# The C row multiplied into the scanned state channel by channel, and sixteen states summed by accumulating transposes, in a two-layer Mamba and MoE kernel

## The chip, the cores and the metric

The kernel runs on one core of a Trainium2 chip. The metric is the device time of one execution in microseconds. Everything is float32.

## The reference, cut to what matters

Two layers. Layer 0 is a selective state space mixer (Mamba) beside a mixture of experts, layer 1 a bilinear attention beside another mixture of experts. The change lies in layer 0's mixer, with 4 sequences of 1024 tokens, 256 inner channels and 16 states:

```
xc = silu(causal_conv4(xs) + conv_b)              # per channel, over time
dbl = xc @ W_x                                    # 64 dt columns | 16 B columns | 16 C columns
dt = softplus(dbl[:, :64] @ W_dt + b_dt)
h_t[d, n] = exp(dt_t[d] * A[d, n]) * h_{t-1}[d, n] + dt_t[d] * xc_t[d] * B_t[n]
y_t[d]    = sum over n of h_t[d, n] * C_t[n]
out       = ((y + xc * D_param) * silu(z)) @ W_out
```

So per state n: one recurrence over time for each channel, then a multiplication by a number that depends on the token and n but not on the channel, and a sum over the 16 states.

## The kernel before, in words

One program for the five engines, each walking the same list, `plan` (made by `make_plan`), and issuing its share of each entry in that order. Nothing is reordered at run time, so an engine that waits holds up all that stands behind it in the list.

The mixer is cut into 8 chunks q (`CH`) of 512 tokens (`HALF`). A chunk has 16 steps, one per state n, so there are 128 steps N = 16 q + n (`STEPS`). Channels lie on the partitions, in two halves k of 128. Each step:

- ScalarE (`decay`, L827) writes the decays exp(dt * A) of step N + 1 into `pA` in PSUM, one 128x512 operation per half, as soon as the scan of step N has read that half (`h_ready`). After the scan of an even chunk it copies the last column of `h` into `carry` (L961).
- GpSimd (L648) multiplies `dtx` with the B row of the state into `dBx`, 128x1024, two steps deep. It waits for the scan of two steps earlier (L646). The B rows come by DMA, broadcast to all partitions, two states to a transfer (`b_group`, L837), issued by ScalarE.
- VectorE (`scan`, L1151) runs the recurrence, one `tensor_tensor_scan` of 128x512 per half, from `pA` (PSUM) and `dBx` (SBUF) to `h` (SBUF).
- TensorE (`hflip`, L734) transposes the 8 blocks of `h` into `pH` (two PSUM banks), tokens on partitions. In that layout C is a per-partition scalar, taken from `ct`.
- VectorE (`sum`, L1164) adds `pH * ct` to `acc` in SBUF: four 128x256 operations. This comes one step later: the sum of step N - 1 stands behind the scan of step N.

At a chunk boundary (step 16 q) the last sum is followed by `accT` (L748: TensorE transposes `acc` back, 8 blocks, into `pH`), and then by `y` (L1186: VectorE, two 128x512 operations that read `pH`, and one 128x1024 operation with both inputs in SBUF) and `mix_out`. The `hflip` of that step waits for `y_ready`, since `pH` is in use.

Around these, each step carries work of the mixtures of experts in two lanes, a (layer 0, later also 1) and b (layer 1, from step 55). A slot of a lane is `gate` (VectorE: two operations, L1210 and L1217), `up` (TensorE matmuls, ScalarE tanh L976 or L981) and `flip` (TensorE transposes and the down projection into `pM`; ScalarE copies `yj`, L988, and `hT`, L991). Some steps have a second slot of lane a, called c. The order within a step is written out at the top: `WITH_SECOND` and `WITH_ONE`. Behind it come the step's extras (`at(...)`): convolution, softplus, norms, routing, gathers and the combination of expert rows. `ct` is such an extra: 8 small matmuls into `pM` and a ScalarE copy. All uses of the one bank `pM` take turns (`take`, `bank_full`, `bank_read`).

Of the kernel before, what the change touches and what calls it, by code (L numbers as in the profile page):

```python
# [7 lines left out]
ALU = mybir.AluOpType  # L8
# [3 lines left out]
P = 128  # L12
NB, L = 4, 1024
CT = L // P
HALF = 512
# [13 lines left out]
GB = 2  # L29
NG = NS // GB  # L30
# [3 lines left out]
WITH_SECOND = "a scan b sum c hflip".split()  # L34
WITH_ONE = "a scan b sum hflip".split()
# [27 lines left out]
def make_plan():  # L63
# [33 lines left out]
    def mixer_front(q, s):  # L97
# [7 lines left out]
        at(s + 6, "ct", q)  # L105
# [56 lines left out]
    for b in range(NB):  # L162
# [16 lines left out]
        for piece in range(len(pieces(1, b))):  # L179
# [5 lines left out]
            ("soft", 0), ("ln", 0), ("ct", 0), ("dt", 0)]  # L185
# [28 lines left out]
    for step in range(max(end + 3, max(extras) + 1)):  # L214
# [5 lines left out]
        for what in order:  # L220
# [29 lines left out]
def program(nc, T, out):  # L250
# [10 lines left out]
    for it in plan:  # L261
        if it[0] in ("xT", "logits", "rank", "xs", "dbl", "ct", "dtr", "z", "mix_out", "gram", "pm", "wm", "attn"):
# [27 lines left out]

    carries = [sum((m // NS) % 2 == 0 for m in range(N + 1)) for N in range(STEPS)]

    with ExitStack() as ctx:
# [85 lines left out]
        dbl = sb("dbl", [R + NS, HALF])  # L379
# [4 lines left out]
        ct = sb("ct", [P, 2, HT, NS])  # L384

        bcb = sb("bcb", [P, 2, GB, HALF])
        dBx = sb("dBx", [P, 2, DK, HALF])
        h = sb("h", [P, 2, DK, HALF])
        carry = sb("carry", [P, DK, NS])
        acc = sb("acc", [P, HT, DI])  # L390
        y = sb("y", [P, DK, HALF])

# [12 lines left out]
        b_rows = [dram(f"b_rows{q}", (NS, HALF)) for q in range(CH)]  # L405
# [25 lines left out]
        def tj_of(i, k):  # L431
# [19 lines left out]
        b_loaded = [sem("b_loaded0"), sem("b_loaded1")]  # L451
        y_ready, accT_full = sem("y_ready"), sem("accT_full")
        decay_ready, dBx_ready, h_ready, hflip_full, sum_done, carried = (
            sem("decay_ready"), sem("dBx_ready"), sem("h_ready"), sem("hflip_full"), sem("sum_done"), sem("carried"))
# [47 lines left out]
        def _(sp):  # L502
            for kind, *a in plan:
# [18 lines left out]
                elif kind == "dbl":  # L522
                    q, = a
                    sp.wait_ge(bank_read, use["dbl", q])
                    sp.dma_start(b_rows[q], dbl[R:R + NS, :]).then_inc(rows_stored, 16)
# [56 lines left out]
        def _(pool):  # L582
            for kind, *a in plan:
# [50 lines left out]
                elif kind in ("decay", "scan"):  # L634
# [5 lines left out]
                    G = N // GB  # L640
                    if n == 0:
                        pool.wait_ge(dtx_ready, q + 1)
                    if N % GB == 0:
                        pool.wait_ge(b_loaded[G % 2], 16 * (G // 2 + 1))
# [7 lines left out]
        def _(pe):  # L652
# [11 lines left out]
            for kind, *a in plan:  # L664
# [48 lines left out]
                elif kind == "dbl":  # L713
# [3 lines left out]
                    for k in range(DK):  # L717
                        last = mm(pM[0:R + NS, :], w_x[:, k, 0:R + NS], xc[q % 2][:, k, :], start=(k == 0), stop=(k == DK - 1))
                    last.then_inc(bank_full, 1)
                elif kind == "ct":  # L720
                    q, = a
                    take("ct", q)
                    for c in range(HT):
                        for k in range(DK):
                            last = mm(pM[:, c * NS:(c + 1) * NS], xc[q % 2][:, k, c * P:(c + 1) * P], w_x[:, k, R + NS:],
                                      start=(k == 0), stop=(k == DK - 1))
# [559 lines left out]
```

## Time and profile before

| | |
|---|---|
| three runs | 1298.37 us median, 1295.57 to 1302.18 |
| the profiled execution | span 1307.9 us, which is all that is recorded of its time |
| VectorE busy | 1017.0 us, 78% of the span |
| TensorE busy | 929.5 us, 71%; weight loads 657.1 us, 50% |
| GpSimd and ScalarE busy | 604.3 us, 46%; 577.0 us, 44% |
| granted TensorE clock, mean | 0.840 |

The page gives the busy time of each engine and groups of instructions by line. A group's busy time counts overlapping instructions once, so it can be less than the mean of one times the count. "Idle before" is the time in which the engine stood still ahead of such an instruction, with the work that ended the wait. The 128 steps lie between 60 us and 1105 us; before them are the loads and the first chunk's front, behind them the rest of layer 1.

### The profile page before, as it was taken

What the parts mean: (1) busy time and instruction counts of PE and PEld (TensorE: products, weight loads), DVE (VectorE), ACT (ScalarE), POOL (GpSimd) and SP (SyncE); (2) the same over time, 40 slices, a digit from 0 to 9 for tenths busy, and PEclk for the clock granted to TensorE, in tenths of its full rate; (3) what the DMA queues carried; (4) which work ended last, traced back from release to release, by engine and by line L of the source; (5) the groups of instructions that cost most, each with busy time, mean ns of one, the idle gap of its engine ahead of it and who ended that gap; (6) DMA issues with size and microseconds to landing.
All of it is one profiled execution on the core that took longest, in us unless ns stands there. A gap on an engine that the chain in (4) does not pass through costs nothing. (4 is left out here: it accounts for less than half of the span.)

```text
span 1307.9 us, 16996 instructions
## 1 busy us (share of the span) xinstructions
PE 929.5 (71%) x4484; PEld 657.1 (50%) x4484; DVE 1017.0 (78%) x2059; ACT 577.0 (44%) x1499; POOL 604.3 (46%) x416
## 2 busy tenths in 40 slices
PE   1467788776677869777887788776877887563680
PEld 0244465554455646554664565564645665432350
DVE  4398889899988998888979987889788998341333
ACT  1333545453446544644555554544464464221320
POOL 0238225675335434673255324864656363423405
PEclk9996789978888978988989998887987899675755
DMA  8812112133112212333222222343422332411404
GB/s 266 231 41 89 44 54 87 62 107 110 56 54 77 79 48 74 92 113 105 64 71 84 73 68 67 97 115 87 117 86 71 110 115 73 121 44 61 135 24 113
DMA packets 149770, 117.19 MB, mean 90 GB/s; under 512 B 15104, under 2 KB 137008, under 8 KB 149680
## 3 DMA queue, kind: packets, MB, share of 16 engines
q1 hardware_dynamic: 132272, 65.76, 17.8%
q10 hardware_dynamic: 9216, 33.56, 7.8%
q0 software_dynamic: 8192, 16.79, 4.0%
q8 instruction: 41, 0.67, 0.2%
q14 instruction: 49, 0.40, 0.1%
HBM read 76.74 MB, written 39.32 MB: 89 GB/s over the span
## 5 line engine op out<-in xcount | busy, mean ns | idle before, releaser
L648 POOL TENSOR_TENSOR dBx<-dtx,bcb 128x1024 f32<-128x1024 f32 x128 | 303.4, 2373 | 398.1 <-DVE h L1162 333.6
L1183 DVE SCALAR_TENSOR_TENSOR acc<-pH,ct,acc 128x256 f32<-128x256 f32 x480 | 197.3, 472 | 4.7 <-remote 3.3
L746 PE MATMUL pH<-const,h 128*128 128x128 f32 x1024 | 160.2, 303 | 43.9 <-DVE h L1162 15.1
L808 PE MATMUL pM<-const,hj 128*128 128x128 f32 (+3 forms) x588 | 125.3, 314 | 75.2 <-ACT hT L991 30.8
L620 POOL DMA_INDIRECT gy<-rows_out,slots x128 | 128.3, 1003 | 99.9 <-DMA rows_out<-yj 63.4
L607 POOL DMA_INDIRECT rows_in<-xn,slots x128 | 132.8, 1038 | 90.2 <-DVE expert L1108 58.3
L1162 DVE TENSOR_TENSOR_SCAN h<-pA,carry,dBx 128x512 f32<-128x512 f32 x128 | 157.0, 1268 | 19.9 <-ACT pA L835 13.6
L835 ACT ACTIVATE pA<-dt,am 128x512 f32<-128x512 f32 x256 | 167.3, 695 | 5.2 <-DVE h L1162 5.1
L1162 DVE TENSOR_TENSOR_SCAN h<-pA,dBx 128x512 f32<-128x512 f32 x128 | 149.2, 1207 | 20.9 <-ACT pA L835 12.0
L746 PEld LDWEIGHTS pH<-const,h 128*128 128x128 f32 x1024 | 126.8, 155 | 65.0 <-issue 27.8
L988 ACT ACTIVATE yj<-pM 128x128 f32<-128x128 f32 x248 | 69.3, 279 | 193.7 <-PE pM L818 170.7
L808 PEld LDWEIGHTS pM<-const,hj 128*128 128x128 f32 (+3 forms) x588 | 73.0, 148 | 152.1 <-issue 121.6
L794 PE MATMUL pG<-w13a,xgT 128*128 x184 | 88.1, 565 | 69.6 <-DVE hj L1217 65.9
L818 PE MATMUL pM<-w2b,hT 128*128 (+1 forms) x496 | 117.9, 341 | 7.1 <-ACT hT L991 4.9
L1210 DVE SCALAR_TENSOR_TENSOR hj<-tj,pG 128x352 f32<-128x352 f32 (+2 forms) x147 | 65.8, 448 | 68.0 <-ACT tj L981 41.4
L991 ACT ACTIVATE hT<-pM 128x256 f32<-128x256 f32 (+1 forms) x248 | 104.6, 422 | 0.5 <-PE pM L808 0.2
L818 PEld LDWEIGHTS pM<-w2b,hT 128*128 128x128 f32 x496 | 86.8, 218 | 33.8 <-issue 18.0
L818 PE MATMUL pM<-w2a,hT 128*128 x552 | 85.1, 295 | 0.0
L795 PE MATMUL pU<-w13a,xgT 128*128 x184 | 82.6, 535 | 0.0
L818 PEld LDWEIGHTS pM<-w2a,hT 128*128 128x128 f32 x552 | 78.5, 214 | 0.3
L794 PEld LDWEIGHTS pG<-w13a,xgT 128*128 128x128 f32 x184 | 32.4, 217 | 91.5 <-issue 91.1
L976 ACT ACTIVATE tj<-pG 128x352 f32<-128x352 f32 x92 | 42.8, 465 | 80.8 <-PE pG L794 68.1
(172 smaller groups left out, 1510.3 us busy)
## 6 DMA issues: line engine op xcount, KB each, us to landing
bcb<-b_rows ACTq DMA_DIRECT2D x64, 512.0 KB
rows_out<-yj SPq DMA_DIRECT2D x248, 64.0 KB
xg<-rows_in SPq DMA_DIRECT2D x184, 64.0 KB
rows_in<-gy SPq DMA_DIRECT2D x8, 512.0 KB, 5.6
mixed<-s_st SPq DMA_DIRECT2D x16, 256.0 KB
so<-rows_out SPq DMA_DIRECT2D x8, 512.0 KB
sr<-mixed SPq DMA_DIRECT2D x8, 512.0 KB
w13a<-in_L_ffn_w SPq DMA_DIRECT2D x2, 1408.0 KB, 8.1
```

The costliest lines, as they stand in the source:

```text
L607: pool.indirect_dma_start(rows_in[l][b % 2], bass.IndirectOffsetOnAxis(ap=slots[l][b][:, c, k:k + 1], axis=0), xn[:, c, :], None).then_inc ...
L620: pool.indirect_dma_start(gy[:, k, c, :], None, rows_out[l][b], bass.IndirectOffsetOnAxis(ap=slots[l][b][:, c, k:k + 1], axis=0)).then_inc ...
L648: pool.tensor_tensor(dBx[:, N % 2], dtx[q % 2][:], row, ALU.mult).then_inc(dBx_ready, 1)
L746: last = pe.transpose(pH[:, half, c * DI + k * P:c * DI + (k + 1) * P], h[:, N % 2, k, t * P:(t + 1) * P], ident)
L794: mm(pG[:, 0:hid], tok, w[:, 0:hid], start=True, stop=True).then_inc(gate_full, 1)
L795: mm(pU[:, 0:hid], tok, w[:, hid:2 * hid], start=True, stop=True).then_inc(gu_full[i], 1)
L808: last = pe.transpose(pM[0:w, m * P:(m + 1) * P], hj[i][:, k % 2, m * P:m * P + w], ident)
L818: last = mm(pM[:, YA:YA + P], hT[i][0:wd, m * P:(m + 1) * P], w[0:wd, m, :], start=(m == 0), stop=(m == len(ks) - 1))
L835: A(pA[:, k, :], dt[q % 2][:, k, :], ACT.Exp, scale=am[:, k, n:n + 1]).then_inc(decay_ready, 1)
L991: last = A(hT[i][:, 0:w], pM[:, 0:w], ACT.Copy)
L1162: dve.tensor_tensor_scan(h[:, N % 2, k, :], pA[:, k, :], dBx[:, N % 2, k, :], carry[:, k, n:n + 1] if q % 2 else 0.0, ALU.mult, ALU.add).t ...
L1183: last = dve.scalar_tensor_tensor(out=acc[:, t, :], in0=src, scalar=cn, in1=acc[:, t, :], op0=ALU.mult, op1=ALU.add)
```

## The change

- The C rows are stored to DRAM beside the B rows, and a transfer per step brings both rows of one state, broadcast to all partitions, into a ring of three (`BCR`). Before, one transfer brought the B rows of two states. A step now moves 512 KB instead of 256 KB, in 128 instead of 64 issues from ScalarE's queue. `ct` with its matmuls and copy goes.
- The scan writes in place, over `pA`. Behind each half's scan VectorE waits for it and multiplies the half by the C row into `hc`, one 128x512 operation. The `sum` entry goes.
- `hflip` transposes `hc` with accumulation: the 16 states of a chunk add up in `pH`. TensorE no longer waits for sums, and VectorE no longer reads `pH` in each step.
- ScalarE's decay of step N + 1 waits for the multiplication (`hc_ready`) instead of the scan, and in even chunks it first copies the last column of each half out of `pA`, with a wait for that copy.
- At the boundary, `accT` moves from the place of the sum to the place ahead of `y`, behind slot c. ScalarE copies the 128x1024 sums from `pH` to SBUF (over `y`, once `zsilu` has read it), TensorE transposes them back, and `y` follows as before.

```diff
-WITH_SECOND = "a scan b sum c hflip".split()
-WITH_ONE = "a scan b sum hflip".split()
+WITH_SECOND = "a scan b c hflip".split()
+WITH_ONE = "a scan b hflip".split()
...
-        at(s + 6, "ct", q)
...
-            elif what == "sum" and 0 < step <= STEPS:
-                plan.append(("sum", step - 1))
-                if n == 0:
-                    plan.append(("accT", q - 1))
             elif what == "hflip":
                 if step and n == 0 and step <= STEPS:
+                    plan.append(("accT", q - 1))
                     plan.append(("y", q - 1))
...
-                    row = bcb[:, G % 2, N % GB:N % GB + 1, :].broadcast_to([P, DK, HALF])
+                    row = bcb[:, N % BCR, 0:1, :].broadcast_to([P, DK, HALF])
...
-                    pe.wait_ge(h_ready, 2 * (N + 1))
+                    pe.wait_ge(hc_ready, 2 * (N + 1))
                     if n == 0 and q:
                         pe.wait_ge(y_ready, q)
                     for half in range(2):
-                        if N:
-                            pe.wait_ge(sum_done, 2 * (N - 1) + half + 1)
                         for c in range(2):
                             for k in range(DK):
                                 t = 2 * half + c
-                                last = pe.transpose(pH[:, half, c * DI + k * P:c * DI + (k + 1) * P], h[:, N % 2, k, t * P:(t + 1) * P], ident)
-                        last.then_inc(hflip_full, 1)
+                                last = mm(pH[:, half, c * DI + k * P:c * DI + (k + 1) * P], hc[:, N % 2, k, t * P:(t + 1) * P], ident,
+                                          is_transpose=True, start=(n == 0 and c == k == 0), stop=(n == NS - 1), skip_group_check=True)
+                    last.then_inc(hflip_full, 1)
                 elif kind == "accT":
                     q, = a
-                    pe.wait_ge(sum_done, 2 * NS * (q + 1))
+                    pe.wait_ge(acc_copied, q + 1)
...
+                keeps = N and (N - 1) // NS % 2 == 0
                 for k in range(DK):
                     if N:
-                        act.wait_ge(h_ready, 2 * (N - 1) + k + 1)
+                        act.wait_ge(hc_ready, 2 * (N - 1) + k + 1)
+                    if keeps:
+                        A(carry[:, k, (N - 1) % NS:(N - 1) % NS + 1], pA[:, k, HALF - 1:HALF], ACT.Copy).then_inc(carried, 1)
+                        act.wait_ge(carried, 2 * ((N - 1) // (2 * NS) * NS + (N - 1) % NS) + k + 1)
                     A(pA[:, k, :], dt[q % 2][:, k, :], ACT.Exp, scale=am[:, k, n:n + 1]).then_inc(decay_ready, 1)
...
+            def bc_load(N):
+
+                q, n = divmod(N, NS)
+                if n == 0:
+                    act.wait_ge(rows_stored, 16 * (q + 1))
+                if N >= BCR:
+                    act.wait_ge(dBx_ready, N - BCR + 1)
+                    act.wait_ge(hc_ready, 2 * (N - BCR + 1))
+                src = bc_rows[q].rearrange("(w n) t -> n w t", w=2)[n:n + 1]
+                act.dma_start(bcb[:, N % BCR], src.broadcast_to([P, 2, HALF])).then_inc(bc_loaded[N % BCR], 16)
...
+                elif kind == "accT":
                     q, = a
+                    act.wait_ge(hflip_full, NS * (q + 1))
+                    act.wait_ge(zs_ready, q + 1)
+                    A(yT.rearrange("p c d -> p (c d)"), pH[:].rearrange("p h t -> p (h t)"), ACT.Copy).then_inc(acc_copied, 1)
...
                     if N >= 2:
-                        dve.wait_ge(hflip_full, 2 * (N - 1))
-                        dve.wait_ge(carried, carries[N - 2])
...
+                        dve.wait_ge(hflip_full, N - 1)
                     for k in range(DK):
                         dve.wait_ge(decay_ready, 2 * N + k + 1)
-                        dve.tensor_tensor_scan(h[:, N % 2, k, :], pA[:, k, :], dBx[:, N % 2, k, :],
+                        dve.tensor_tensor_scan(pA[:, k, :], pA[:, k, :], dBx[:, N % 2, k, :],
                                                carry[:, k, n:n + 1] if q % 2 else 0.0, ALU.mult, ALU.add).then_inc(h_ready, 1)
-                elif kind == "sum":
...
+                        dve.wait_ge(h_ready, 2 * N + k + 1)
+                        dve.tensor_tensor(hc[:, N % 2, k, :], pA[:, k, :], bcb[:, N % BCR, 1, :], ALU.mult).then_inc(hc_ready, 1)
```

## Rows read from the trace of the kernel before

**Rows 1.** Windows, the steps: length, PE, PEld, DVE, ACT, POOL busy, clock, DMA, GB/s.

```profile
60.00:1105.00 1045.00, 807.53 (x4055) 578.96 (x4056) 922.15 (x1827) 517.88 (x1329) 534.46 (x344) 0.87 0.26 81
```

**Rows 2.** Waits of VectorE from 60 to 1105 us: total, times, longest us.

```profile
DVE h L1162 <- ACT pA L835: 25.6, 26, 2.1
...
DVE h L1162 <- PE pH L746: 3.4, 1, 3.4
```

**Rows 3.** Groups by line and shape, VectorE: busy us, mean ns, idle before.

```profile
L1183 DVE SCALAR_TENSOR_TENSOR acc<-pH,ct,acc 128x256 f32<-128x256 f32 x480 | 197.3, 472 | 4.7 <-remote 3.3 <-PE pH L746 1.3
L1162 DVE TENSOR_TENSOR_SCAN h<-pA,carry,dBx 128x512 f32<-128x512 f32 x128 | 157.0, 1268 | 19.9 <-ACT pA L835 13.6 <-issue 3.2 <-POOL dBx L648 3.0
L1162 DVE TENSOR_TENSOR_SCAN h<-pA,dBx 128x512 f32<-128x512 f32 x128 | 149.2, 1207 | 20.9 <-ACT pA L835 12.0 <-POOL dBx L648 4.8 <-PE pH L746 3.4
L1217 DVE TENSOR_TENSOR hj<-hj,pU 128x352 f32<-128x352 f32 x92 | 47.9, 521 | 10.3 <-ACT xgT L969 5.4 <-remote 1.4 <-PE pU L795 0.8
...
L1217 DVE TENSOR_TENSOR hj<-hj,p 128x176 f32<-128x176 f32 x78 | 26.3, 337 | 2.7
...
L1191 DVE SCALAR_TENSOR_TENSOR y<-xc,dpar,pH 128x512 f32<-128x512 f32 x16 | 11.2, 744 | 8.6 <-PE pH L753 8.2 <-issue 0.3
```

**Rows 4.** Timeline of VectorE, one step: start us, length us, instructions.

```profile
607.73 2.33 DVE L1162 TENSOR_TENSOR_SCAN h<-pA,dBx 128x512 f32<-128x512 f32 x2
609.98 1.63 DVE L1183 SCALAR_TENSOR_TENSOR acc<-pH,ct,acc 128x256 f32<-128x256 f32 x4
```

**Rows 5.** Line L725, the matmuls of `ct`, in the groups of TensorE.

```profile
L725 PE MATMUL pM<-w_x,xc 128*128 128x16 f32 x128 | 16.9, 275 | 0.8 <-ACT v L928 0.8
```

**Rows 6.** Timelines of ScalarE behind slot c and of VectorE at `y`, step 16.

```profile
195.07 0.48 ACT L991 ACTIVATE hT<-pM 128x384 f32<-128x384 f32 x1
...
190.70 1.41 DVE L1191 SCALAR_TENSOR_TENSOR y<-xc,dpar,pH 128x512 f32<-128x512 f32 x2 [0.21 <-PE pH L753]
192.14 1.22 DVE L1194 SCALAR_TENSOR_TENSOR y<-y,zs 128x1024 f32<-128x1024 f32 x1
```

**Rows 7.** Timeline of TensorE at step 16: `accT`, `hflip`, `mix_out`.

```profile
189.56 1.09 PE L753 MATMUL pH<-const,acc 128*128 128x128 f32 x8 [2.31 <-DVE acc L1183]
...
194.70 1.04 PE L746 MATMUL pH<-const,h 128*128 128x128 f32 x8
195.70 2.02 PE L761 MATMUL pM<-w_out,y 128*128 128x128 f32 x16
```

**Rows 8.** Timelines at step 96: ScalarE behind slot c, VectorE, GpSimd.

```profile
862.15 0.48 ACT L991 ACTIVATE hT<-pM 128x384 f32<-128x384 f32 x1
...
859.55 1.41 DVE L1191 SCALAR_TENSOR_TENSOR y<-xc,dpar,pH 128x512 f32<-128x512 f32 x2 [0.31 <-issue]
860.99 6.67 DVE L1194 SCALAR_TENSOR_TENSOR y<-y,zs 128x1024 f32<-128x1024 f32 x1
...
860.07 1.92 POOL L629 TENSOR_TENSOR gy<-gy,wts 128x1024 f32<-128x1024 f32 x1
861.93 2.35 POOL L648 TENSOR_TENSOR dBx<-dtx,bcb 128x1024 f32<-128x1024 f32 x1
864.23 2.35 POOL L633 TENSOR_TENSOR gy<-gy 128x1024 f32<-128x1024 f32 x1
```

**Rows 9.** Groups of ScalarE: the decays, and an operation of 128x1024.

```profile
L835 ACT ACTIVATE pA<-dt,am 128x512 f32<-128x512 f32 x256 | 167.3, 695 | 5.2 <-DVE h L1162 5.1
...
L933 ACT ACTIVATE ca<-v 128x1024 f32<-128x1024 f32 x8 | 8.5, 1060 | 0.3
```

**Rows 10.** Timelines at step 112, which has no slot c: ScalarE, VectorE.

```profile
1010.82 0.38 ACT L991 ACTIVATE hT<-pM 128x256 f32<-128x256 f32 x1
...
1012.55 0.75 DVE L1191 SCALAR_TENSOR_TENSOR y<-xc,dpar,pH 128x512 f32<-128x512 f32 x1 [3.84 <-PE pH L753]
```

**Rows 11.** Timeline of VectorE at step 64: the last operation of `y`.

```profile
580.56 4.20 DVE L1194 SCALAR_TENSOR_TENSOR y<-y,zs 128x1024 f32<-128x1024 f32 x1
```

**Rows 12.** Waits of GpSimd from 60 to 1105 us.

```profile
POOL dBx L648 <- DVE h L1162: 333.6, 70, 10.6
```

More of the change, by code:

```diff
@@ L261, in program @@
     for it in plan:
-        if it[0] in ("xT", "logits", "rank", "xs", "dbl", "ct", "dtr", "z", "mix_out", "gram", "pm", "wm", "attn"):
+        if it[0] in ("xT", "logits", "rank", "xs", "dbl", "dtr", "z", "mix_out", "gram", "pm", "wm", "attn"):
             takes(*it)
@@ L289, in program @@
     wide_before = [sum(2 * HID[j[0], j[2]] > 512 for j in lanes[0][:k]) for k in range(len(lanes[0]) + 1)]
-    carries = [sum((m // NS) % 2 == 0 for m in range(N + 1)) for N in range(STEPS)]
     with ExitStack() as ctx:
@@ L378, in program @@
         v = sb("v", [P, DK, HALF])
-        dbl = sb("dbl", [R + NS, HALF])
+        dbl = sb("dbl", [R + 2 * NS, HALF])
         zs = sb("zs", [P, DK, HALF])
@@ L403, in dram @@
             return nc.dram_tensor(name, shape, F32, kind="Internal").ap()
-        b_rows = [dram(f"b_rows{q}", (NS, HALF)) for q in range(CH)]
+        bc_rows = [dram(f"bc_rows{q}", (2 * NS, HALF)) for q in range(CH)]
         rows_in = [[dram(f"rows_in{l}{i}", (TILES * P, P)) for i in range(2)] for l in range(2)]
@@ L450, in program @@
             sem("rows_stored"), sem("act_chain"), sem("ln_ready"), sem("dt_ready"), sem("dtx_ready"))
-        b_loaded = [sem("b_loaded0"), sem("b_loaded1")]
+        bc_loaded = [sem(f"bc_loaded{i}") for i in range(BCR)]
         y_ready, accT_full = sem("y_ready"), sem("accT_full")
-        decay_ready, dBx_ready, h_ready, hflip_full, sum_done, carried = (
-            sem("decay_ready"), sem("dBx_ready"), sem("h_ready"), sem("hflip_full"), sem("sum_done"), sem("carried"))
+        decay_ready, dBx_ready, h_ready, hc_ready, hflip_full, carried = (
+            sem("decay_ready"), sem("dBx_ready"), sem("h_ready"), sem("hc_ready"), sem("hflip_full"), sem("carried"))
+        zs_ready, acc_copied = sem("zs_ready"), sem("acc_copied")
         mixed_stored, gathered, fetched, combined, mid_stored, out_stored = (
@@ L717, in _ @@
                     for k in range(DK):
[L718 to L726, printed above, removed]
+                        last = mm(pM[0:R + 2 * NS, :], w_x[:, k, :], xc[q % 2][:, k, :], start=(k == 0), stop=(k == DK - 1))
                     last.then_inc(bank_full, 1)
@@ L745, in _ @@
                                 t = 2 * half + c
[L746 to L747 removed]
+                                last = mm(pH[:, half, c * DI + k * P:c * DI + (k + 1) * P], hc[:, N % 2, k, t * P:(t + 1) * P], ident,
+                                          is_transpose=True, start=(n == 0 and c == k == 0), stop=(n == NS - 1), skip_group_check=True)
+                    last.then_inc(hflip_full, 1)
                 elif kind == "accT":
                     q, = a
[L750 removed]
+                    pe.wait_ge(acc_copied, q + 1)
                     for k in range(DK):
                         for c in range(HT):
[L753 removed]
+                            last = pe.transpose(pH[:, k, c * P:(c + 1) * P], yT[:, c, k * P:(k + 1) * P], ident)
                     last.then_inc(accT_full, 1)
@@ L947, in _ @@
                 elif kind == "decay":
-                    b_group(0)
-                    b_group(1)
+                    for N in range(BCR):
+                        bc_load(N)
                     act.wait_ge(prepared, 2)
@@ L956, in _ @@
                         decay(N + 1)
-                    if N % GB == GB - 1 and N // GB + 2 < CH * NG:
-                        b_group(N // GB + 2)
-                    if q % 2 == 0:
-                        act.wait_ge(h_ready, 2 * N + 2)
-                        A(carry[:, :, n], h[:, N % 2, :, HALF - 1], ACT.Copy).then_inc(carried, 1)
+                    if N + BCR < STEPS:
+                        bc_load(N + BCR)
                 elif kind == "up":
@@ L1149, in _ @@
                     dve.wait_ge(bank_read, use["z", q, 1])
-                    link(dve.scalar_tensor_tensor(out=zs[:], in0=zs[:], scalar=1.0, in1=y[:], op0=ALU.add, op1=ALU.mult))
+                    dve.scalar_tensor_tensor(out=zs[:], in0=zs[:], scalar=1.0, in1=y[:], op0=ALU.add, op1=ALU.mult).then_inc(zs_ready, 1)
+                    dve.wait_ge(zs_ready, q + 1)
                 elif kind == "scan":
@@ L1154, in _ @@
                     dve.wait_ge(dBx_ready, N + 1)
+                    if q % 2:
+                        dve.wait_ge(carried, 2 * (q // 2 * NS + n + 1))
                     if N >= 2:
[L1156 to L1159 removed]
+                        dve.wait_ge(hflip_full, N - 1)
                     for k in range(DK):
                         dve.wait_ge(decay_ready, 2 * N + k + 1)
[L1162 removed]
+                        dve.tensor_tensor_scan(pA[:, k, :], pA[:, k, :], dBx[:, N % 2, k, :],
                                                carry[:, k, n:n + 1] if q % 2 else 0.0, ALU.mult, ALU.add).then_inc(h_ready, 1)
[L1164 to L1185 removed]
+                        dve.wait_ge(h_ready, 2 * N + k + 1)
+                        dve.tensor_tensor(hc[:, N % 2, k, :], pA[:, k, :], bcb[:, N % BCR, 1, :], ALU.mult).then_inc(hc_ready, 1)
                 elif kind == "y":
```

53 lines of the change are left out of this document (8 added, 45 removed).

## The prediction, made before the changed kernel was built or run

> **What bounds the kernel now.** I read the windows first. In the stretch of the 128 steps, 1045 us of the 1307.9, VectorE is busy for 922.2 us, 88%, and TensorE for 807.5 us, 77%, at a mean granted clock of 0.87 [rows 1]. So VectorE sets the pace, with 122.8 us of idle time, about 1 us per step, and TensorE is not far behind. Its granted clock moves between the two levels of 1.2 and 2.4 GHz. Next come VectorE's waits. The largest is for the decays (25.6 us), and the wait that the round trip through TensorE causes is small, 3.4 us [rows 2]. The four sum operations cost VectorE their own time, not a wait. The groups give that time [rows 3], and the timeline of a step shows the order in which it is spent [rows 4].
>
> **VectorE's own work.** The sums are 512 operations: 197.3 us for 480 of them, 0.411 us each with their overlap [rows 3]. In a step they take 1.63 us [rows 4], of which 0.08 us overlaps with a neighbour, since the sum starts at 609.98 and the scans end at 610.06. That is 1.55 us per step, 198 us in all.
>
> Two multiplications per step come in, 128x512, one input in PSUM, one in SBUF. None of this shape is in the trace. The nearest rows are `tensor_tensor` at L1217, also one input in each: 521 ns for 352 elements and 337 ns for 176, so 1.045 ns per element and 153 ns fixed, 688 ns for 512. From above it is bounded by L1191, 512 elements with a per-partition scalar besides, 744 ns, and from below by the busy time per element alone, 535 ns [rows 3]. I take 688 ns, as its rows have the same operation. The two scans of a step overlap by 0.07 us (2.33 us for two of 1.20) [rows 3, 4]. Each multiplication must wait for its own scan, so that overlap goes. I allow 0.05 us per step for it and the waits together. Added: 2 x 0.688 + 0.05 = 1.43 us per step, 183 us. Net: **-15 us**. With 535 ns it would be -54, with 744 ns 0.
>
> The Trainium skill (VectorE: DVE Perf Modes, section on the TRN2 errata) has a table by which an operation out of PSUM takes 120 cycles plus its elements at 0.96 GHz, 658 ns here, and beside it a measured (N + 151)/0.96 for fp32 `tensor_tensor`, 691 ns. The trace's slope and constant agree with the second. By the table alone this term would be 8 us lower.
>
> The scan now writes to PSUM instead of SBUF. The trace has no scan that does. Nearest is what an extra operand costs a scan, 1268 against 1207 ns with `carry` [rows 3]. So I bound it by -0.06 and +0.06 us for each of 256 scans, 16 us either way, and take 0.
>
> **Round trips.** VectorE no longer waits for `hflip` before a sum nor TensorE for the sum: 3.4 us of VectorE's idle time [rows 2], and TensorE gets ahead by a little. I take **-5 us** (bounds 0 and -10). The `ct` matmuls take 16.9 us of TensorE [rows 5] with a turn of `pM`. TensorE is not what ends most waits, so **-3 us** (bounds 0 and -17).
>
> ScalarE is 50% busy [rows 1]. Its decay now waits for the multiplication. That is covered: the first half's decay runs while VectorE does the second half's scan and multiplication (1.9 us), against a decay of 0.7 us [rows 9] and a copy of one column. If the cover fails, the price is the 25.6 us row growing. The added issues for B and C rows (64 more) are also on its queue, behind the decay. The transfers double by 33.5 MB in a DMA system that is 26% busy [rows 1]. They are wanted two steps later. I take 0 for both, and +10 us as the upper bound.
>
> **The boundary.** Before, `accT` stood ahead of slot c, and `y` could run as soon as gate c was done: at step 16 it waited 0.21 us and started at 190.70 [rows 6]. Now TensorE's `accT` waits for a ScalarE copy that stands behind all of slot c in ScalarE's queue. That slot can only run after gate c. ScalarE's last copy for it ended at 195.55 at step 16 [rows 6], 4.85 us behind `y`'s old start, and at step 96 at 862.63, 3.08 us behind 859.55 [rows 8]. Six boundaries have a slot c (16, 32, ... 96), and over the six this mean is 3.2 us. To it come the copy, 1.06 us as another 128x1024 operation [rows 9], the 8 transposes, 1.09 us [rows 7], and 0.15 us of handing over. 0.3 us comes off, since `accT` no longer stands ahead of slot c in TensorE. So VectorE waits 5.2 us at each of six boundaries, **31 us**, with nothing to do, because the extras and the next gate stand behind `y` in its queue. TensorE waits too: `hflip`, which ran at 194.70 without a wait [rows 7], has to wait for `y`.
>
> Steps 112 and 128 have no slot c. At 112, ScalarE's copies end at 1011.20, and `y` started at 1012.55 after a wait of 3.84 us [rows 10]. Copy, transposes (up to twice 1.09 us, at the lower of the two clock levels) and the handing over put it at about 1014.5, 1.9 us later. The sum's 1.6 us that I have counted as gained were hidden there, so 3.5 us each, **7 us**.
>
> Against it: at steps 64 and 96 the last operation of `y` took 4.20 and 6.67 us [rows 8, 11], where it takes 1.22 at step 16 [rows 6]. It ended 1.08 us after the third of GpSimd's operations did [rows 8]. Started 5 us later it would not meet them: **-8 us**. And after a long wait of VectorE the other engines are ahead, so the next waits shrink: **-4 us**. Boundary in all: **+26 us**, bounds +10 and +41.
>
> **Contention with GpSimd.** The same row shows the rule: a VectorE operation with both inputs in SBUF stands still while GpSimd multiplies. The sums, with one input in PSUM, kept their 472 ns. GpSimd's `dBx` takes 2.35 us [rows 8] and starts at the end of a scan in 70 of 128 steps [rows 12]. The sums covered 1.63 us of it with work that does not mind. The multiplications cover 0.69, the second half's, so 0.94 us more of it falls on what comes next. About 50 steps have an extra with both inputs in SBUF there (convolution two steps per chunk, `xc`, `dt`, `zsilu`, the norms, the combinations): 50 x 70/128 x 0.94 = 26 us, of which I take three quarters, **+20 us**, for the waits that it shortens in turn. Bounds 0 and 47 (all 50 steps).
> The Trainium skill (SBUF — State Buffer, "Who interferes with whom") calls this an exclusive lock that the first comer holds for its whole instruction. By that the multiplication itself, with one input in SBUF, is free of it, and all 26 us would be paid, 6 more than I take.
>
> **Lane b.** Gate b stands behind the scans, so it comes 1.43 us later, and TensorE's work for b then runs into slot c. Eleven steps have both (56, 60, ... 96). At most 1.43 us each, 16 us. I take **+5 us**.
>
> Sum: -15 - 5 - 3 + 26 + 20 + 5 = +28 us on the profiled 1307.9 us. Its span is 9.5 us (0.7%) above the median of the runs, 1298.37. I carry the difference over to the median: **1326 us**.
>
> **Rivals.**
> *A, the waits are refunded (faster).* VectorE has 123 us of idle time in the steps [rows 1]. If what the boundary, lane b and GpSimd cost comes back as shorter waits for decays and tanh within the next steps, only -15 - 5 - 3 = -23 us are left: 1275 us. It decides once 5 us of boundary wait are made good within five steps of 1 us idle each. For it: after a boundary wait TensorE and ScalarE are ahead. Against it: TensorE stands still for `y` as well. Chance 0.20.
> *D, half refunded.* Half of the 51 us comes back: 1300 us, no change. Chance 0.14.
> *B, the scan in PSUM costs.* +16 us for the scans, and the whole 26 us of contention, +6, and half of the bound for DMA and ScalarE, +5: 1353 us. For it: three accesses in PSUM and SBUF per element. Against: reading from PSUM showed no extra in rows 3. Chance 0.12.
> *C, the accumulating transposes run as full matmuls.* The change would then not do what it says, a transpose. 8 transposes take 1.04 us, while the 8 matmuls of `mix_out`, of the same size, are 16 records in 2.02 us [rows 7]: +0.98 us per step on TensorE, 125 us, of which its idle time hides about half. 1326 + 62 = 1388 us. The Trainium skill (Perfetto Trace Analysis, "Transposes") says that transposes have logic that skips arithmetic. The operands here are the same as before, only the accumulation differs. Chance 0.04.
> *Forecast.* 1326 us, own range 1308 to 1345. Chance 0.50.
>
> No change means within 0.5% of 1298.37, 1292 to 1305, about what runs can tell. Faster is A, 0.20. Same is D, 0.14. Slower is the rest, 0.66. The range takes in half of A and all but C and the upper part of B: 1284 to 1354 us.
>
> **What the changed profile would show.** The multiplication at 0.69 us, 256 times. Scans at 1.20 and 1.27 us. `y` preceded by 4 to 6 us of idle time on VectorE at six boundaries, released by `accT`. `hflip` with 8 records of a transpose's length. VectorE's busy time about equal to 1017 us, its idle time in the steps up by some 25 us. Convolution, `xc` and norm operations longer than before by what falls into `dBx`. The prediction is wrong if the boundaries show less than 2 us of wait, if the two-input operations are no longer than before, or if scan and multiplication together take clearly less than 3.7 us a step.

## The result, and the profile after

The changed kernel takes 1344.71 us (median of 4 runs, 1340.59 to 1351.45), the kernel before on the same chip 1296.97 us: a ratio of **1.037 [1.0328, 1.0412]**, slower, 48 us. I had forecast 1326 us, slower, with 1308 to 1345 as my own range, so the time stands at its very edge. Chips differ by over 1% (the kernel before took 1315 us on another), so every experiment below is a ratio to the kernel before on its own chip: runs 1 to 4 shared one chip, 5 to 8 a second, 9 to 12 a third. The ratios leave out one execution of run 1 (1397.69 us) and one of run 8 (1303.07 us) that fell in a slower state.

The page of the kernel after, its span and busy times:

```profile
span 1345.6 us, 16371 instructions
## 1 busy us (share of the span) xinstructions
PE 913.9 (68%) x4356; PEld 648.3 (48%) x4356; DVE 1032.6 (77%) x1803; ACT 598.9 (45%) x1563; POOL 606.8 (45%) x416
```

Its stretch of the 128 steps, columns as in rows 1:

```profile
60.00:1145.00 1085.00, 790.23 (x3901) 569.64 (x3902) 929.66 (x1559) 534.69 (x1378) 538.70 (x344) 0.86 0.43 108
```

The steps take 1085 us where they took 1045 [rows 1]. VectorE is busy for 7.5 us more in them (929.7 against 922.2) and idle for 32.5 us more (155.3 against 122.8). Over the whole span VectorE's busy time is 1032.6 us against 1017.0. The groups of VectorE (busy us, mean ns, idle before, and what ended it) say what of it is new:

```profile
L1150 DVE TENSOR_TENSOR hc<-pA,bcb 128x512 f32<-128x512 f32 x256 | 177.0, 692 | 8.8
L1147 DVE TENSOR_TENSOR_SCAN pA<-pA,carry,dBx 128x512 f32<-128x512 f32 x128 | 164.4, 1285 | 22.2 <-POOL dBx L639 14.3 <-ACT pA L821 5.9 <-ACT carry L819 1.9
L1147 DVE TENSOR_TENSOR_SCAN pA<-pA,dBx 128x512 f32<-128x512 f32 x128 | 156.6, 1223 | 27.0 <-ACT pA L821 19.5 <-POOL dBx L639 7.3
L1107 DVE SCALAR_TENSOR_TENSOR ca<-xs,cw,ca 128x512 f32<-128x512 f32 x48 | 53.3, 1112 | 11.9 <-ACT ca L893 10.8
...
L1135 DVE SCALAR_TENSOR_TENSOR zs<-zs,y 128x1024 f32<-128x1024 f32 x8 | 23.7, 2967 | 0.0
L1117 DVE SCALAR_TENSOR_TENSOR xc<-v,ca 128x1024 f32<-128x1024 f32 x8 | 20.2, 2521 | 1.1 <-ACT v L899 1.1
...
L1156 DVE SCALAR_TENSOR_TENSOR y<-xc,dpar,pH 128x512 f32<-128x512 f32 x16 | 11.2, 744 | 52.2 <-PE pH L735 52.2
...
L1159 DVE SCALAR_TENSOR_TENSOR y<-y,zs 128x1024 f32<-128x1024 f32 x8 | 10.6, 1320 | 0.3
```

The same groups of the kernel before, where they are not among its rows above:

```profile
L1122 DVE SCALAR_TENSOR_TENSOR ca<-xs,cw,ca 128x512 f32<-128x512 f32 x48 | 43.0, 897 | 11.9 <-ACT ca L906 10.8
...
L1150 DVE SCALAR_TENSOR_TENSOR zs<-zs,y 128x1024 f32<-128x1024 f32 x8 | 19.0, 2369 | 3.0 <-ACT y L946 3.0
L1194 DVE SCALAR_TENSOR_TENSOR y<-y,zs 128x1024 f32<-128x1024 f32 x8 | 18.2, 2278 | 0.3
L1132 DVE SCALAR_TENSOR_TENSOR xc<-v,ca 128x1024 f32<-128x1024 f32 x8 | 14.2, 1774 | 1.1 <-ACT v L912 1.1
```

The multiplication takes 692 ns, 256 times, 177.0 us. The scans are 16 ns longer each than in rows 3, and have 321.0 us of busy time against 306.2. Convolution (L1107), `zsilu` (L1135) and `xc` (L1117) read both inputs from SBUF and grew by 10.3, 4.7 and 6.0 us, with unchanged counts. `y*zs` (L1159), which reads both from SBUF too, fell by 7.6 us. Ahead of `y` (L1156) there are now 52.2 us of idle time, where rows 3 have 8.6.

The timeline of VectorE at step 16 (start us, length us, idle time before in brackets) shows one of the eight waits that make these 52.2 us, and ScalarE and TensorE at the same place show what it waits for:

```profile
196.23 1.29 DVE L1147 TENSOR_TENSOR_SCAN pA<-pA,carry,dBx 128x512 f32<-128x512 f32 x1 [1.43 <-ACT carry L819]
197.56 0.69 DVE L1150 TENSOR_TENSOR hc<-pA,bcb 128x512 f32<-128x512 f32 x1
198.17 1.28 DVE L1147 TENSOR_TENSOR_SCAN pA<-pA,carry,dBx 128x512 f32<-128x512 f32 x1
...
200.63 0.52 DVE L1182 TENSOR_TENSOR hj<-hj,pU 128x352 f32<-128x352 f32 x1
209.81 1.41 DVE L1156 SCALAR_TENSOR_TENSOR y<-xc,dpar,pH 128x512 f32<-128x512 f32 x2 [8.65 <-PE pH L735]
211.25 1.23 DVE L1159 SCALAR_TENSOR_TENSOR y<-y,zs 128x1024 f32<-128x1024 f32 x1
```

```profile
206.35 0.48 ACT L976 ACTIVATE hT<-pM 128x384 f32<-128x384 f32 x1
206.72 1.03 ACT L910 ACTIVATE y<-pH 128x1024 f32<-128x1024 f32 x1
...
207.80 1.97 PE L735 MATMUL pH<-const,y 128*128 128x128 f32 x8 [1.67 <-ACT y L910]
212.62 0.66 PE L727 MATMUL pH<-const,hc 128*128 128x128 f32 x2 [2.85 <-DVE y L1159]
```

Gate c is VectorE's last work before the wait (200.63 plus 0.52). ScalarE's `hT` of slot c ends at 206.83, the copy at L910 runs until 207.75, then the transposes at L735, and `y` starts at 209.81. The eight idle times are 8.65, 5.55, 7.16, 5.58, 6.65, 6.58, 7.04 and 4.98 us. They were 0.21, 1.45, 0.20, 0.23, 0.54, 0.31, 3.84 and 1.78.

The waits of VectorE, then those of GpSimd, from 60 to 1145 us (total, times, longest), and the queue and the issue that load the B and C rows (packets, MB, share; KB, us to landing):

```profile
DVE y L1156 <- PE pH L735: 47.2, 7, 8.7
DVE pA L1147 <- ACT pA L821: 25.4, 21, 3.5
DVE pA L1147 <- POOL dBx L639: 21.6, 7, 6.5
```

```profile
POOL dBx L639 <- DVE pA L1147: 272.2, 49, 16.5
POOL dBx L639 <- DMA bcb<-bc_rows: 180.7, 37, 44.6
```

```profile
q10 hardware_dynamic: 34816, 67.12, 22.1%
...
bcb<-bc_rows ACTq DMA_DIRECT2D x128, 512.0 KB, 5.1
```

The same wait and the same queue in the kernel before:

```profile
POOL dBx L648 <- DMA bcb<-b_rows: 62.5, 7, 42.9
...
q10 hardware_dynamic: 9216, 33.56, 7.8%
```

The wait for decays has not moved (25.6 us in rows 2). The rows were the last thing that GpSimd's product waited for 7 times, and are now 37 times, 180.7 us in all. The queue has 22.1% where it had 7.8%. The bytes doubled, but the packets went from 9216 to 34816: two neighbouring B rows lay in one run of 4 KB, and a state's B row and C row lie apart, in runs of 2 KB. So the change also halved the length of the runs.

### The profile page after: what moved, and what is told of

Same layout as the page of the kernel before. It is cut to its first block and busy times, and to the rows that moved or that the text cites. A ratio compares the mean times of both kernels' runs of the same rounds, so it can differ in the third digit from the quotient of the medians.

```text
span 1345.6 us, 16371 instructions
## 1 busy us (share of the span) xinstructions
PE 913.9 (68%) x4356; PEld 648.3 (48%) x4356; DVE 1032.6 (77%) x1803; ACT 598.9 (45%) x1563; POOL 606.8 (45%) x416
## 3 DMA queue, kind: packets, MB, share of 16 engines
q10 hardware_dynamic: 34816, 67.12, 22.1%
q1 hardware_dynamic: 132400, 66.02, 17.3%
## 5 line engine op out<-in xcount | busy, mean ns | idle before, releaser
L727 PE MATMUL pH<-const,hc 128*128 128x128 f32 x1024 | 162.3, 310 | 74.9 <-DVE hc L1150 53.9
L1150 DVE TENSOR_TENSOR hc<-pA,bcb 128x512 f32<-128x512 f32 x256 | 177.0, 692 | 8.8
L1147 DVE TENSOR_TENSOR_SCAN pA<-pA,carry,dBx 128x512 f32<-128x512 f32 x128 | 164.4, 1285 | 22.2 <-POOL dBx L639 14.3
L821 ACT ACTIVATE pA<-dt,am 128x512 f32<-128x512 f32 x256 | 172.9, 693 | 15.4 <-DVE hc L1150 11.1
L1147 DVE TENSOR_TENSOR_SCAN pA<-pA,dBx 128x512 f32<-128x512 f32 x128 | 156.6, 1223 | 27.0 <-ACT pA L821 19.5
L727 PEld LDWEIGHTS pH<-const,hc 128*128 128x128 f32 x1024 | 131.5, 159 | 94.7 <-DVE hc L1150 63.2
L600 POOL DMA_INDIRECT rows_in<-xn,slots x128 | 135.7, 1060 | 73.6 <-DVE expert L1093 41.7
L790 PE MATMUL pM<-const,hj 128*128 128x128 f32 (+3 forms) x588 | 123.8, 311 | 52.2 <-DVE hj L1182 32.8
L776 PEld LDWEIGHTS pG<-w13a,xgT 128*128 128x128 f32 x184 | 32.1, 215 | 102.4 <-issue 101.9
```

Source lines behind the costliest of these rows:

```text
L600: pool.indirect_dma_start(rows_in[l][b % 2], bass.IndirectOffsetOnAxis(ap=slots[l][b][:, c, k:k + 1], axis=0), xn[:, c, :], None).then_inc ...
L727: last = mm(pH[:, half, c * DI + k * P:c * DI + (k + 1) * P], hc[:, N % 2, k, t * P:(t + 1) * P], ident, is_transpose=True, start=(n == 0 ...
L776: mm(pG[:, 0:hid], tok, w[:, 0:hid], start=True, stop=True).then_inc(gate_full, 1)
L790: last = pe.transpose(pM[0:w, m * P:(m + 1) * P], hj[i][:, k % 2, m * P:m * P + w], ident)
L821: A(pA[:, k, :], dt[q % 2][:, k, :], ACT.Exp, scale=am[:, k, n:n + 1]).then_inc(decay_ready, 1)
L1147: dve.tensor_tensor_scan(pA[:, k, :], pA[:, k, :], dBx[:, N % 2, k, :], carry[:, k, n:n + 1] if q % 2 else 0.0, ALU.mult, ALU.add).then_in ...
```

## The experiments

**1. `accT` early.** The copy and `accT` are planned ahead of slot c, as `accT` was before.

```diff
-WITH_SECOND = "a scan b c hflip".split()
+WITH_SECOND = "a acc scan b c hflip".split()
...
+            elif what == "acc":
+                if step and n == 0 and step <= STEPS:
+                    plan.append(("accT", q - 1))
```

> The changed kernel with one edit: accT (ScalarE's copy of the sums and TensorE's transposes back) stands ahead of the scan in the boundary step instead of behind slot c. Theory (the boundary wait is the largest part of the loss): the idle time ahead of y, 52.2 us in the changed kernel and 8.6 before, falls to under 12 us, and most of it, 25 to 40 us, comes off the total: 1305 to 1320 us. Rival A (boundary waits are made good within some steps): the idle time goes and the total stays within 8 us of 1345.

Measured: 1306.16 us, 1.0073 [1.0042, 1.0103]. Its groups of VectorE:

```profile
L1161 DVE SCALAR_TENSOR_TENSOR y<-y,zs 128x1024 f32<-128x1024 f32 x8 | 21.6, 2702 | 0.3
...
L1158 DVE SCALAR_TENSOR_TENSOR y<-xc,dpar,pH 128x512 f32<-128x512 f32 x16 | 11.2, 744 | 8.7 <-PE pH L737 8.6
```

`y` waits 8.7 us, as before the change, and `y*zs` is back in GpSimd's way, 21.6 us. The net is 1.037 less 1.0073, 3.0%: **38 us of the 48 are the boundary**, as my theory for the run had it (25 to 40 us).

**2. GpSimd's product in halves.** Each half waits for its own half of the scan, so it starts one scan earlier and holds SBUF in shorter pieces.

```diff
-                    if N >= 2:
-                        pool.wait_ge(h_ready, 2 * (N - 1))
-                    row = bcb[:, N % BCR, 0:1, :].broadcast_to([P, DK, HALF])
-                    pool.tensor_tensor(dBx[:, N % 2], dtx[q % 2][:], row, ALU.mult).then_inc(dBx_ready, 1)
+                    for k in range(DK):
+                        if N >= 2:
+                            pool.wait_ge(h_ready, 2 * (N - 2) + k + 1)
+                        pool.tensor_tensor(dBx[:, N % 2, k, :], dtx[q % 2][:, k, :], bcb[:, N % BCR, 0, :], ALU.mult).then_inc(dBx_ready, 1)
```

> The changed kernel with one edit: GpSimd's dBx product is made in two halves of 512, each half once the scan of two steps earlier has read that half. Half of it then runs beside the multiplication and the second scan, which have at most one input in SBUF, and only some 0.5 us instead of 1.7 us runs beside what follows. Theory (contention with GpSimd's product costs about 34 us of VectorE's busy time): convolution (53.3 us), xc (20.2) and zs (23.7) get shorter, in all 15 to 25 us off the total, 1320 to 1330. Rival: those operations are long because of GpSimd's other work, or stalls there are slack: within 5 us of 1345.

Measured: 1322.61 us, 1.0203 [1.0165, 1.024]. The page and two groups:

```profile
PE 901.5 (68%) x4356; PEld 641.5 (49%) x4356; DVE 1000.5 (76%) x1803; ACT 599.5 (45%) x1563; POOL 635.1 (48%) x544
...
L1107 DVE SCALAR_TENSOR_TENSOR ca<-xs,cw,ca 128x512 f32<-128x512 f32 x48 | 44.6, 931 | 11.9 <-ACT ca L893 10.8
...
L1117 DVE SCALAR_TENSOR_TENSOR xc<-v,ca 128x1024 f32<-128x1024 f32 x8 | 15.3, 1909 | 1.1 <-ACT v L899 1.1
```

VectorE's busy time falls by 32.1 us, and convolution and `xc` go back nearly to what they were before the change (43.0 and 14.2 us). That looked like a measure of the contention that the change exposed, until run 6.

**3. Rows side by side.** A state's B row and C row lie next to each other in DRAM, so the same bytes go in runs of 4 KB instead of 2, as they did before the change.

```diff
-        bc_rows = [dram(f"bc_rows{q}", (2 * NS, HALF)) for q in range(CH)]
+        bc_rows = [dram(f"bc_rows{q}", (NS, 2, HALF)) for q in range(CH)]
```

> The changed kernel with one edit: B row and C row of a state lie side by side in DRAM (stored by two DMAs per chunk), so a broadcast moves 4 KB runs instead of 2 KB runs, same bytes. Theory (the DMA term, taken as nothing in the prediction, is real: GpSimd waits 181 us for the rows, and VectorE 21.6 us for dBx against 7.8): the queue's share falls from 22% to about 15%, the transfers land sooner than 5.1 us, the wait of VectorE for dBx falls under 14 us, total 5 to 12 us lower, 1333 to 1340. Rival (DMA is hidden by the two steps of lead): same time within 4 us.

Measured: 1343.56 us, 1.0348 [1.0297, 1.0398], no difference from the kernel after. GpSimd's wait for rows fell to 102.1 us, 19 times, and VectorE's for `dBx` only to 17.9, where my theory had under 14. The page's queue and issue:

```profile
q10 hardware_dynamic: 18432, 67.12, 15.2%
...
bcb<-bc_rows ACTq DMA_DIRECT2D x128, 512.0 KB, 3.8
```

**4. Thin rows.** From the fourth step on only 16 of 128 partitions are loaded with B and C.

```diff
-                act.dma_start(bcb[:, N % BCR], src.broadcast_to([P, 2, HALF])).then_inc(bc_loaded[N % BCR], 16)
+                p = P if N < BCR else 16
+                act.dma_start(bcb[0:p, N % BCR], src.broadcast_to([p, 2, HALF])).then_inc(bc_loaded[N % BCR], 16)
```

> The changed kernel with one edit: from the fourth step on, only 16 of the 128 partitions of the B and C rows are loaded (the others keep what the first three loads brought, so the sums are not the reference's). It leaves out seven eighths of the added and the old row traffic. If waiting for rows and DMA load cost something, this is its upper bound: GpSimd's waits for the rows go from 181 us to about the 43 us of the start, VectorE's wait for dBx to under 9 us, total 10 to 20 us lower (1325 to 1335). Rival (hidden): within 4 us of 1345.

Measured: 1331.91 us, 1.0257 [1.0222, 1.0291]. This kernel's output is not the reference's. All but an eighth of the row traffic, the old B rows' share included, is worth 1.1%, 12 us below run 3 and 15 by the two ratios (their intervals leave 8 to 22). VectorE's wait for `dBx` stays at 20.5 us, so rows that come late are not its cause. VectorE's busy time is 10 us lower, 1022.5, and GpSimd hardly ever finds the rows late:

```profile
POOL dBx L639 <- DVE pA L1148: 386.5, 76, 17.3
POOL dBx L639 <- DMA bcb<-bc_rows: 51.6, 4, 44.3
```

**5 and 6. Both edits together, and the split in the kernel before.** Run 5 is 1 and 2 in one kernel. Run 6 has edit 2 alone in the kernel before the change.

> The changed kernel with both edits of the first runs: accT ahead of the scan, and GpSimd's product in halves. Theory (boundary wait and contention are separate losses and add): 1345 - 38 - 22 = 1285 us, 0.6 to 1.3% faster than the kernel before. Rival (they share idle time, so that the second gains little): 1298 to 1305 us.

> The kernel before, with GpSimd's product in halves and nothing else. It tells how much of that gain the old order had already: there the sums, 1.63 us with one input in PSUM, lay beside the product. Theory (the change exposed it): 3 to 12 us faster than before, clearly less than the 22 us in the changed kernel; 1285 to 1294 us. Rival (the gain has nothing to do with the change): some 20 us faster, 1275 to 1280 us.

Measured: 1296.79 us, 0.9856 [0.9821, 0.9892], and 1293.78 us, 0.9839 [0.981, 0.9869]. The losses add (3.0% and 1.7% alone, 5.1% together), and with both edits the changed kernel is faster than the one before. But the split gives the kernel before 1.6% too, and my theory had 3 to 12 us for it. With the same split on both sides, 0.9856 against 0.9839, the changed kernel has no lead. The page of run 6 has VectorE 17.6 us less busy than in the kernel before (1017.0):

```profile
PE 925.6 (72%) x4484; PEld 656.6 (51%) x4484; DVE 999.4 (78%) x2059; ACT 576.8 (45%) x1499; POOL 625.9 (49%) x544
```

So what edit 2 gains is mostly contention that was there all along, and run 2 is no measure of the change.

**7. The kernel before with `accT` late.** Only the place in the order is changed, with no ScalarE copy.

```diff
                 plan.append(("sum", step - 1))
-                if n == 0:
-                    plan.append(("accT", q - 1))
...
                 if step and n == 0 and step <= STEPS:
+                    plan.append(("accT", q - 1))
                     plan.append(("y", q - 1))
```

> The kernel before, with accT behind slot c (ahead of y) instead of behind the sum, as the changed kernel has it, but with no ScalarE copy in its way. It shows the price of TensorE's place alone. By the timelines TensorE finishes slot c 2.4 to 4.2 us behind the old start of y, then the transposes take 1.1 us: y waits 3.5 to 5 us at six boundaries, idle time ahead of y 25 to 30 us instead of 8.6. Theory (place in the queues is the loss): 15 to 25 us slower than before, 1312 to 1322 us. Rival (the ScalarE copy is what costs): within 8 us of before.

Measured: 1333.73 us, 1.0119 [1.0078, 1.016], some 15 us. VectorE's row:

```profile
L1190 DVE SCALAR_TENSOR_TENSOR y<-xc,dpar,pH 128x512 f32<-128x512 f32 x16 | 11.2, 744 | 31.7 <-PE pH L752 31.7
```

The place alone makes 23.1 us of idle time (31.7 less 8.6). The other 20.5 of the 52.2 I put down to the copy, which lengthens the chain and ties it to ScalarE's queue. No run has the late copy alone. Run 1 has the copy in the early place, and there `y` waits no longer than before the change.

**8. All three edits.** Runs 1, 2 and 3 in one kernel.

> As the run with both edits, and the B and C rows of a state side by side in DRAM as well. Theory (once the boundary wait is gone, the transfers' landing time still does not end a wait of VectorE): within 4 us of that run. Rival (rows are needed sooner once the rest is faster): 5 to 12 us below it.

Measured: 1279.97 us, **0.9723 [0.9694, 0.9753]**, the fastest of all. Its page:

```profile
span 1278.6 us, 16635 instructions
## 1 busy us (share of the span) xinstructions
PE 887.6 (69%) x4356; PEld 628.7 (49%) x4356; DVE 993.4 (78%) x1803; ACT 599.8 (47%) x1563; POOL 634.8 (50%) x544
```

Against run 5 on the same chip the rows side by side gain 1.3%, where alone (run 3) they gained nothing. The kernel before has runs of 4 KB already, so run 6 is its fair counterpart: 0.9723 against 0.9839, 1.2%, is what the change gains once order, rows and product are alike.

**9. The kernel before without the cover of the sums.** GpSimd's product also waits for the sums that follow the scan, so what it covers is VectorE's next work.

```diff
                         pool.wait_ge(h_ready, 2 * (N - 1))
+                    if N >= 3:
+                        pool.wait_ge(sum_done, 2 * (N - 2))
```

> The kernel before, with GpSimd's product made to wait for the sums of the step as well, so that nothing of them lies beside it. It asks for the full price of the cover that the prediction said the sums give: the product then starts 1.6 us later and all its 2.36 us lie beside what follows. Theory (cover by work with one input in SBUF is worth time): VectorE's operations with both inputs in SBUF rise from 241 us to 275 or more, total 20 to 45 us slower than before, ratio 1.015 to 1.035. Rival (such stalls fall into slack): under 8 us, ratio within 1.006.

Measured: 1322.24 us, 1.0178 [1.0145, 1.0212], 23 us, inside my theory's range. Page and convolution (43.0 us and 897 ns in the kernel before):

```profile
PE 931.0 (70%) x4484; PEld 658.1 (50%) x4484; DVE 1051.8 (80%) x2059; ACT 577.1 (44%) x1499; POOL 617.1 (47%) x416
...
L1124 DVE SCALAR_TENSOR_TENSOR ca<-xs,cw,ca 128x512 f32<-128x512 f32 x48 | 61.8, 1289 | 11.9 <-ACT ca L908 10.8
```

**10. `accT` early, product later.** Run 1, where the product also waits for the multiplication behind the scan, 0.75 us more with the hand-over.

```diff
-                        pool.wait_ge(h_ready, 2 * (N - 1))
+                        pool.wait_ge(hc_ready, 2 * (N - 1))
```

> The changed kernel with accT ahead of the scan (ratio to before 1.0073 alone), and GpSimd's product waiting for the multiplication of the second half instead of its scan, so it starts some 0.75 us later. Theory: a smaller dose of the same, operations with both inputs in SBUF rise from 277 us by 10 to 20, total 6 to 15 us above that run, ratio 1.012 to 1.019. Rival (slack): within 4 us, ratio 1.004 to 1.010.

Measured: 1316.53 us, 1.0165 [1.013, 1.0199], 0.9% or 12 us over run 1. VectorE is busy for 1051.6 us (1035.7 in run 1):

```profile
PE 894.7 (68%) x4356; PEld 632.3 (48%) x4356; DVE 1051.6 (80%) x1803; ACT 600.9 (46%) x1563; POOL 611.9 (47%) x416
```

Runs 9 and 10 are two prices of the same thing: work out of PSUM that stands beside GpSimd's product. 1.63 us per step of it are worth 23 us, 0.75 us are worth 12. The change took 0.94 us away (1.63 of the sums, less 0.69 of the second multiplication). By the first that is 13 us, by the second 15, if the rest of what delays the product were the same.

**11 and 12. The near rows with one of the other edits.** Run 11 is 1 and 3, run 12 is 2 and 3.

> The changed kernel with accT ahead of the scan, and B and C rows side by side in DRAM, product not split. The rows side by side gave nothing alone (ratio 1.0348 against 1.037) and 1.3% with both other edits. Theory S (it is the split that asks for rows sooner): ratio near 1.007, as without them. Theory B (it is the missing boundary wait): ratio 0.990 to 0.998.

> The changed kernel with GpSimd's product in halves (ratio 1.0203 alone) and B and C rows side by side in DRAM, accT left where the change put it. Theory S (it is the split that asks for rows sooner: its run has 263 us of GpSimd waiting for them): ratio 1.005 to 1.012. Theory B (it is the missing boundary wait): ratio near 1.020.

Measured: 1298.75 us, 1.0010 [0.9986, 1.0033], and 1317.7 us, 1.0149 [1.0121, 1.0177]. The gain over run 1 is 0.6%, over run 2 0.5%, neither of them 0 nor the 1.3% of run 8. The intervals of run 2 and run 12 overlap, so the second is weakly shown. Neither theory holds clean.

**All pairs side by side.** The first column is the busy time of VectorE's `tensor_tensor` and `scalar_tensor_tensor` groups with both inputs in SBUF, added up from the profiles: 224.7 us in the kernel before, 253.9 in the changed one, 260.3 in run 1. The second is the difference of the two ratios, in us.

| pair, one edit apart | two-input groups | time |
|---|---|---|
| run 9 against before | +32.4 | +23 |
| run 10 against run 1 | +10.2 | +12 |
| run 3 against after | +1.7 | -3 |
| run 11 against run 1 | -0.7 | -8 |
| run 12 against run 2 | -6.6 | -7 |
| run 4 against after | -9.7 | -15 |
| run 8 against run 5 | -14.7 | -17 |
| run 6 against before | -17.3 | -21 |
| run 2 against after | -28.6 | -22 |
| run 5 against run 1 | -28.9 | -28 |

Each group time comes from one execution, so a few us mean nothing. Even so, the edits to the product and to the rows moved the time about as far as they moved these operations.

## Why the prediction was right in sign and short in size

- **What bounds the kernel.** Right. VectorE's work and waits gave the sign, and nothing shows TensorE as the bound (790.2 us busy in the 1085 us of the steps). All three signs of being wrong stayed away: waits of 5 to 9 us at the boundaries, longer two-input operations, and 3.89 us a step for scan and multiplication.
- **Own work, -15.** The multiplication was right: 692 ns against 688, and the 120-cycle table of the Trainium skill (VectorE: DVE Perf Modes, section on the TRN2 errata; 658 ns) does not fit the measured 692. VectorE's sums went (210.4 us of busy time), the multiplications (177.0) and 14.8 us of scans came: -18.6 us.
- **Scan in PSUM, 0 with 16 either way.** 16 ns each, 4 us in busy records. Rival B's first part is out. The other 11 of the 14.8 are overlap lost, where I had allowed 0.05 us per step, 6 us.
- **Round trips, -8; ScalarE, 0.** The wait for decays is unchanged, as forecast. The small gains were not tested alone.
- **Boundary, +26: the term that was mis-sized.** The mechanism was exact: `y` behind the copy behind slot c. Run 1 gives 38 us. At the six boundaries with slot c the idle time rose by 37.2 us (40.2 against 2.9), and I had 31. From the start of the copy to `y` it took 2.4 us on average, close to my 2.3. What remains, 3.8 us behind the old start of `y`, is slot c, where I had 3.2 and took off 0.3 that did not come. At steps 112 and 128 it rose by 6.4 us, where I had 3.8 and 3.2 for the sums besides. `y*zs` gave back 7.6 us (forecast 8). The refund of 4 us does not show: taking the wait away removed 43.5 us of idle time and let `y*zs` grow again by 11, a net of 32.5, and gave back 38. My bounds of +10 and +41 hold the 38. TensorE stands still with it: in the timeline `hflip` waits 2.85 us for `y`.
- **Contention, +20.** The mechanism was right in the main: the two-input operations grew by 29.2 us, even with `y*zs` 7.6 lower, and those that read PSUM did not. But one with a single input in SBUF grew as well, `xs<-ca`, from 10.6 to 12.8 us, and I had not counted such work. How much of this reaches the end is an estimate in each case. By the time for which the product is uncovered, runs 9 and 10 give 13 to 15 us, less than my 20. By what the two-input groups grew, run 9 (23 us for 32.4) and run 10 (12 for 10.2) make it 21 to 34. The 26 us that the exclusive lock of the Trainium skill (SBUF — State Buffer, "Who interferes with whom") would make if all were paid lie between them. The trace agrees with the lock in rows 8, where `y*zs` ends 1.08 us after GpSimd does. It does not agree that the first comer keeps it. In the changed kernel an operation of VectorE began 0.58 us ahead of the product and took 3.51 us, where the shortest of its group takes 0.69, while the product took its usual 2.37:

```profile
297.19 3.51 DVE L1124 TENSOR_SCALAR xs<-ca 128x1024 f32<-128x1024 f32 x1
297.77 2.37 POOL L639 TENSOR_TENSOR dBx<-dtx,bcb 128x1024 f32<-128x1024 f32 x1
```

- **DMA, 0: the step that failed.** I said that the rows are wanted two steps later and took nothing, with +10 as the bound for this and ScalarE. By the plan it is one step: the load for step N + 3 waits for the multiplication of step N, and the product of step N + 3 waits only for the scan of step N + 1. From that multiplication to the end of that scan there are less than the 5.1 us of a landing in 33 of 125 steps. I had also counted the bytes and not the shorter runs. So GpSimd found the rows late 37 times instead of 7, and by the timelines its product started within 0.3 us of the scan's end in 50 steps instead of 76 (77 in run 4). With thin rows the two-input groups are 9.7 us shorter too, so a product that starts late and then lies beside more of this work may be how the rows cost time. It is not shown: run 3 has 67 prompt starts, and neither its groups nor its time are shorter. VectorE's wait for `dBx` grew from 7.8 us [rows 3] to 21.6, but thin rows leave it, so it isn't late rows, and its cause stays open. Run 4 gives 12 to 15 us for nearly all the row traffic, more than the change added to it, so that is an upper bound for the change, and its interval doesn't decide whether my +10 was broken.
- **Lane b, +5.** Not seen. The waits for its tanh were 19.6 and 11.6 us before and are 18.7 and 10.9.

Together: boundary 38 and 10 us for all the rest (run 1, 0.7%), where I had 26 and +2. With -19 of own work, some 28 us are left for contention and DMA together, where I had 20, and more if the round trips gave back anything. The 13 to 15 us and the 12 to 15 us from above would make 25 to 30, so no large term need be missing. But the two may overlap, since thin rows made the two-input operations shorter, and no run tells them apart.

The rivals: A, the refund, fell by run 1. D fell with it. B's 1353 us came nearer to the measured 1345 than my 1326, but its first reason is wrong, since the scan costs little. Its other parts, all 26 us of contention and 5 for DMA, were nearer than mine. C is refuted by the transposes:

```profile
L727 PE MATMUL pH<-const,hc 128*128 128x128 f32 x1024 | 162.3, 310 | 74.9 <-DVE hc L1150 53.9 <-DVE y L1159 20.7
```

310 ns is the mean of all records, 303 in the kernel before. What was missing among them is the one that happened: a boundary of its full length with no refund.

**What stays open.** Why the product in halves gains 1.6 or 1.7% in both kernels, and 2.2% from run 1 to run 5, though its gain in two-input work is 17.3 us in the kernel before and 28.6 and 28.9 in the changed one. The near rows gain what the table of pairs would have them gain (nothing alone, 7 us with the split, 17 with both), but for run 11, where 8 us come with no shorter two-input work. Why they shorten it only where the product is split is not shown.

## What to carry to other kernels

When an engine is put between two others at a hand-over, look at what stands ahead of the new instruction in each of the three queues: the copy took 1.03 us and the order made it 5 to 9 us of waiting, eight times, and a change of a few lines in the plan gave back 38 us. Work that is taken off an engine may have been the cover of something, here of a GpSimd operation that stops VectorE's two-input operations, so price what comes to stand there in its place. A transfer has two sizes, its bytes and the length of its runs, and the lead that a ring gives it is read from the waits of both sides, not from the number of buffers. And a change that is slower as it stands can be faster with the order fitted to it: 1.037 became 0.972. Most of that is not the change's own, though: the kernel before reaches 0.984 with the split alone, so compare both with the same remedies.

## What the runs showed of the hardware

- Accumulating fp32 transposes into one PSUM region over 16 states cost the same as plain ones, 310 against 303 ns.
- A `tensor_tensor_scan` of 512 elements that reads and writes the same PSUM tile costs 16 ns more than one that writes to SBUF.
- The same 67.12 MB, broadcast from DRAM in runs of 4 KB instead of 2, took 15.2% instead of 22.1% of the DMA engines' time, and landed after 3.8 instead of 5.1 us.
- Beside GpSimd's product a VectorE operation stood still although it had begun 0.58 us before it, and although it had one input only (`xs<-ca`, 3.51 us against 0.69).
- Making GpSimd wait 0.75 us longer per step slowed the kernel by 12 us: the start of an operation on an engine that is 47% busy was worth as much as a tenth of a microsecond per step on the busiest one.
